# A two-stage macaron block with routed experts: results scattered to token rows, low halves formed on VectorE

## The reference

```
x = x + 0.5 * ffn0(norm(x))         # gate, up 256 -> 1024, silu(gate)*up, down
x = x + attn0(norm(x))              # 16 heads of 128, 4 key heads, window mask, rotary
x = x + 0.5 * ffn0(norm(x))
x = x + 0.5 * moe(norm(x))          # the same weights both times
x = x + attn1(norm(x))              # 16 heads of 16, causal, rotary
x = x + 0.5 * moe(norm(x))
```

## Time and profile before

| | us |
|---|---|
| median of 3 runs (890.39 to 892.46) | 890.73 |
| the profiled execution | 887.51 |
| its span, first to last instruction | 885.7 |
| PE busy (share of span) | 722.8 (82%) |
| DVE busy | 621.2 (70%) |
| ACT busy | 454.4 (51%) |
| POOL busy | 397.9 (45%) |

### The profile page before, as it was taken

How to read it: one execution, slowest core, us unless ns; L and a number is a source line. 1 busy time by engine, 2 the same in 40 slices (tenths; PEclk the granted TensorE clock), 3 DMA queues, 4 the chain that set the end, 5 groups by cost and what they waited for, 6 DMA issues and landing times. The chain is left out here.

```text
span 885.7 us, 17508 instructions
## 1 busy us (share of the span) xinstructions
PE 722.8 (82%) x5515; PEld 487.4 (55%) x5515; DVE 621.2 (70%) x1376; ACT 454.4 (51%) x1033; POOL 397.9 (45%) x401
## 2 busy tenths in 40 slices
PE   6889789999889999698976887664896798758883
PEld 3555357777456777354543555333785685436642
DVE  5989868777867787699756554534888695835535
ACT  3435667787667786364322454224666473314531
POOL 4644856766756665385444420743007301230025
PEclk8999989999999999999988899876898698979986
DMA  9999000000000000300001332200000100023313
GB/s 374 316 418 411 23 0 1 0 0 1 1 1 0 0 0 1 113 1 1 24 25 47 95 99 78 83 19 1 1 2 1 48 2 1 1 84 102 103 58 121
DMA packets 36432, 58.83 MB, mean 66 GB/s; under 512 B 11026, under 2 KB 28562, under 8 KB 35858
## 3 DMA queue, kind: packets, MB, share of 16 engines
q1 hardware_dynamic: 32866, 49.49, 15.5%
q0 software_dynamic: 3072, 8.39, 3.0%
q10 hardware_dynamic: 432, 0.15, 0.1%
HBM read 27.87 MB, written 30.15 MB: 66 GB/s over the span
## 5 line engine op out<-in xcount | busy, mean ns | idle before, releaser
L1458 PE MATMUL PS<-XT,WA 128*128 128x512 f16 x432 | 101.1, 382 | 0.0
L603 POOL TENSOR_TENSOR ARENA<-ARENA,ST 128x512 f32<-128x512 f32 x64 | 66.6, 1041 | 67.8 <-DVE ST L1248 67.8
L714 ACT ACTIVATE ARENA<-T 128x512 f16<-128x512 f32 (+1 forms) x56 | 35.2, 629 | 105.1 <-DVE T L1142 90.8
L1458 PE MATMUL PS<-WA,ARENA 128*128 128x256 f16 (+2 forms) x960 | 70.3, 215 | 15.2 <-DVE ARENA L1151 14.2
L1458 PEld LDWEIGHTS PS<-WA,ARENA 128*128 128x128 f16 x960 | 57.6, 98 | 31.4 <-DVE ARENA L1151 18.8
L1458 PE MATMUL PS<-XT,WC 128*128 128x512 f16 x264 | 67.7, 411 | 6.5 <-DVE T L1135 5.2
L561 POOL DMA_INDIRECT WA<-ys_rows,IDX x16 | 17.3, 1081 | 114.4 <-DMA ys_rows<-WA 110.1
L1458 PEld LDWEIGHTS PS<-XT,WA 128*128 128x128 f16 (+1 forms) x432 | 42.7, 99 | 45.0 <-issue 1.9
L1458 PE MATMUL PS<-KVR,ARENA 128*128 (+1 forms) x384 | 59.3, 283 | 6.4 <-DVE ARENA L1220 4.1
L1228 DVE TENSOR_REDUCE ST<-PS 128x2 f32<-128x512 f32 x64 | 44.0, 687 | 28.8 <-PE PS L1458 28.0
L747 ACT ACTIVATE ARENA<-PS,ST 128x256 f32<-128x256 f32 x128 | 59.4, 471 | 8.6 <-DVE ST L1231 8.4
(11 more groups left out here) (179 smaller groups left out, 1839.2 us busy)
## 6 DMA issues: line engine op xcount, KB each, us to landing
xs_rows<-ROUT SPq DMA_DIRECT2D x1, 9216.0 KB, 26.6
ys_rows<-ROUT SPq DMA_DIRECT2D x1, 9216.0 KB, 48.9
WA<-xs_rows SPq DMA_DIRECT2D x46, 128.0 KB, 2.0
ys_rows<-WA SPq DMA_DIRECT2D x46, 128.0 KB, 1.7
WB<-wb_dram SPq DMA_DIRECT2D x1, 4096.0 KB, 21.8
WC<-wc_dram SPq DMA_DIRECT2D x1, 2304.0 KB, 26.9
WA<-wa_dram SPq DMA_DIRECT2D x4, 512.0 KB, 7.6
WA<-wa_dram SPq DMA_DIRECT2D x1, 2048.0 KB, 13.1
```

The costliest lines, as they stand in the source:

```text
L603: pl.tensor_tensor(pr, pr, rs.broadcast_to([P, 2, S]), ALU.mult).then_inc(norm_done, 1)
L714: sc.activation(HH[r, a, 0, :], T3[r, :], ACT.Copy).then_inc(hid_hi, 1)
L1458: ins = te.matmul(dst, left(a), right(b), start=first and n == 0, stop=last and n == 2, skip_group_check=True)
```

## The change

1. Results go straight to rows by token. Each row of the table now carries two more numbers (ROW = D + 2): the token's first expert and twice its number. POOL scatters a block's results (`results(m, b)`) with one indirect DMA to yt_rows, row 2*token + (0 or 1), the target being made by one VectorE instruction per block (`target`). SP's stores and POOL's 16 gathers go; SP loads YG in four plain DMAs. The tables xs_rows are now two, one per moe, filled before with zeros and free row numbers (FREE); ys_rows and its fill go.
2. VectorE forms all low halves of the shared expert; POOL's share (L535) goes. POOL's scatter of the first half moves to step 1 of glu(2, 0), that of the second half behind glu(2, 0) or glu(3, 0).
3. Routing: slots move to step 5, the block table (`routing_table`) to step 0 of glu(f, 1) and the second half's weights to its step 1; PE's prefix goes behind that step's down.
4. The order within an expert iteration changes on PE, ACT and VectorE.
5. PRE is 3 for the second moe. n splits start at step 4 (N_AT) of glu(1, 0), those left over share glu(1, 1)'s first steps. The d splits stand in every second iteration, i = 2 to 16.

```diff
-PRE = 2
+PRE = {2: 2, 3: 3}
+ROW = D + 2
...
+        DIX = sb("DIX", [P, 24], I32)
+        IDP = sb("IDP", [P, ROWS // P + TT], I32)
+        FREE = sb("FREE", [P, ROWS // P], F32)
...
-        SIXTH = [("g", j) for j in range(JF - JS, E)] + [("n", j) for j in range(JF - 2, E)]
+        SIXTH = [("g", j) for j in range(JF - JS, E)]
+        N_AT = 4
...
-            ORDER += [FIFTH[step]] + ([("n", step - 2)] if step >= 2 else [])
-        ORDER += SIXTH + [("d", j) for j in range(8)]
+            ORDER += [FIFTH[step]] + ([("n", step - N_AT)] if step >= N_AT else [])
+        for step in range(JF):
+            ORDER += SIXTH[step:step + 1] + ([("n", step + JF - N_AT)] if step + JF - N_AT < E else [])
+        ORDER += [("d", j) for j in range(8)]
...
@@ SP @@
-            for table in (XS, YS):
-                sp.dma_start(table.rearrange("(p a r) d -> p a (r d)", p=P, r=4),
-                             ROUT[:, 0:4 * D].rearrange("p (o n) -> p o n", o=1)
-                             .broadcast_to([P, ROWS // P // 4, 4 * D])).then_inc(dma_z, 16)
+            sp.wait_ge(base_set, 5)
+            for table in XS:
+                t3 = table.rearrange("(a p) d -> p a d", p=P)
+                sp.dma_start(t3[:, :, 0:D + 1], ROUT[:, 0:D + 1].rearrange("p (o n) -> p o n", o=1)
+                             .broadcast_to([P, ROWS // P, D + 1])).then_inc(dma_z, 16)
+                sp.dma_start(t3[:, :, D + 1:ROW], FREE[:, :].rearrange("p (a o) -> p a o", o=1),
+                             allow_slow_non_contiguous=True).then_inc(dma_z, 16)
...
+                for b in range(NBK):
                     g = NBK * m + b
-                    at[b] = sp.value_load(TBL[0:1, 1, b:b + 1], min_val=0, max_val=ROWS // P - 1)
+                    row = sp.value_load(TBL[0:1, 1, b:b + 1], min_val=0, max_val=ROWS // P - 1)
                     after(sp, xb_turned, g - 2)
-                    sp.dma_start(XB[:, g % 3, :], XS[ds(at[b] * P, P), :]).then_inc(xb_in[g % 3], 16)
-
-                def store(b):
-                    g = NBK * m + b
-                    sp.wait_ge(ye_copied, g + 1)
-                    sp.dma_start(YS[ds(at[b] * P, P), :], YB[:, g % 3, :]).then_inc(yb_out[g % 3], 16)
-
-                for b in range(NBK + 6):
-                    if b < NBK:
-                        load(b)
-                    if b >= 6:
-                        store(b - 6)
+                    after(sp, dix_done, g - 2)
+                    sp.dma_start(XB[:, g % 3, :], XS[m][ds(row * P, P), :]).then_inc(xb_in[g % 3], 16)
+                for i in range(3):
+                    sp.wait_ge(yb_out[i], 16 * slot_total(i, m))
+                for u in range(NB):
+                    sp.dma_start(YG[u // UPH][:, u % UPH], YT[2 * ROWS + 4 * P * u:2 * ROWS + 4 * P * (u + 1), :]
+                                 .rearrange("(t p k) d -> p t k d", t=2, k=2)).then_inc(gathered[u], 16)
...
@@ POOL @@
-            def gather(m):
...
+            def results(m, b):
+                g = NBK * m + b
+                pool.wait_ge(ye_copied, g + 1)
+                pool.wait_ge(dix_done, g + 1)
+                pl.indirect_dma_start(YT, bass.IndirectOffsetOnAxis(ap=DIX[:, b:b + 1], axis=0), YB[:, g % 3, :], None,
+                                      bounds_check=2 * ROWS + 2 * TOK - 1).then_inc(yb_out[g % 3], 16)
...
             run_glu(pool, 2, 0, glu_step, glu_side)
-            for b in range(8):
-                if b < 4:
-                    prepare1(b)
-                split(*split_d(b))
-            gather(0)
+            scatter(3, 1)
+            for i in range(4):
+                prepare1(i)
+            for b in range(NBK):
+                results(0, b)
+                if 2 <= b < 18 and b % 2 == 0:
+                    split(*split_d(b // 2 - 1))
...
@@ ACT @@
-                if (f, hf) == (1, 0) and j == 2:
+                if (f, hf) == (1, 0) and j == N_AT:
                     act.wait_ge(dma_n, 16 * len(pieces(KH)))
...
                         gate_tanh(i)
+                    if 1 <= i <= NBK:
+                        hidden_high(i - 1)
                     if i >= 2:
                         result(i - 2)
                     if i + 2 < NBK:
                         tokens_high(i + 2)
-                    if 1 <= i <= NBK:
-                        hidden_high(i - 1)
-                    if m == 0 and 2 <= i < 10:
-                        split(*split_d(i - 2))
+                    if m == 0 and 2 <= i < 18 and i % 2 == 0:
+                        split(*split_d(i // 2 - 1))
...
@@ DVE @@
+                link(v.tensor_tensor(SLB, EQ[:, 0], KB[:, 0:E].rearrange("p (o e) -> p o e", o=1)
+                                     .broadcast_to([P, TPH, E]), ALU.mult))
+                first = XN[:, UPH * hf:UPH * hf + UPH, :, D:D + 1].rearrange("p u t n -> p (u t) n")
+                link(v.tensor_reduce(first, SLB, AX.X, ALU.add))
                 v.tensor_copy(IDX[:, :, TPH * hf:TPH * hf + TPH], SF).then_inc(idx_done, 1)
...
-                if not low_on_pool(f, hf):
-                    dve.wait_ge(hid_hi, st + 1)
-                    v.tensor_tensor(HH[r, a, 1, :], T3[r, :], HH[r, a, 0, :], ALU.subtract).then_inc(hid_lo, 1)
+                dve.wait_ge(hid_hi, st + 1)
+                v.tensor_tensor(HH[r, a, 1, :], T3[r, :], HH[r, a, 0, :], ALU.subtract).then_inc(hid_lo, 1)
...
+                def target(b):
+                    g = NBK * m + b
+                    dve.wait_ge(xb_in[g % 3], 16 * (slot_uses(g) + 1))
+                    v.scalar_tensor_tensor(DIX[:, b:b + 1], XB[:, g % 3, D:D + 1], BLK[:, 0, b:b + 1],
+                                           XB[:, g % 3, D + 1:D + 2], ALU.not_equal, ALU.add).then_inc(dix_done, 1)
...
                         hidden(i)
-                    if i + 2 < NBK:
-                        tokens_low(i + 2)
                     if 1 <= i <= NBK:
                         hidden_low(i - 1)
-                    if m == 0 and 2 <= i < 10:
-                        split(*split_d(i - 2))
+                    if i + 2 < NBK:
+                        target(i + 2)
+                        tokens_low(i + 2)
+                    if m == 0 and 2 <= i < 18 and i % 2 == 0:
+                        split(*split_d(i // 2 - 1))
...
@@ PE @@
                         gate_up(i)
+                    if 1 <= i <= NBK:
+                        turn_hidden(i - 1)
                     if i >= 2:
                         project(i - 2)
                     if i + 2 < NBK:
                         turn_tokens(i + 2)
-                    if 1 <= i <= NBK:
-                        turn_hidden(i - 1)
```

More of the change, by code:

```diff
@@ L531, in glu_step @@
                     split(*x)
-                if low_on_pool(f, hf):
-                    pool.wait_ge(hid_hi, st + 1)
-                    r = rows(f, j)
-                    pl.tensor_tensor(HH[r, a, 1, :], T3[r, :], HH[r, a, 0, :], ALU.subtract).then_inc(hid_lo, 1)
             def glu_side(f, hf, j):
@@ L665, in _ @@
             run_glu(pool, 3, 0, glu_step, glu_side)
-            gather(1)
+            scatter(6, 1)
+            for b in range(NBK):
+                results(1, b)
         @block.scalar
@@ L702, in glu_step @@
                 after(act, gated, st)
-                if f >= 2 and hf == 1 and j == PRE:
+                if f >= 2 and hf == 1 and j == PRE[f]:
                     act.wait_ge(gu_gated, NBK * (f - 1))
@@ L1197, in hidden_low @@
                                     HTB[:, g % 2, 0], ALU.subtract).then_inc(htb_lo, 1)
-                tokens_low(0)
-                tokens_low(1)
+                def target(b):
[3 more added lines that the diff above has]
+                                           XB[:, g % 3, D + 1:D + 2], ALU.not_equal, ALU.add).then_inc(dix_done, 1)
+                for b in range(2):
+                    target(b)
+                    tokens_low(b)
                 for i in range(NBK + 2):
@@ L1436, in _ @@
             glu(2, 0)
-            glu(2, 1, (0, PRE))
+            glu(2, 1, (0, PRE[2]))
             expert_blocks(0)
-            glu(2, 1, (PRE, JS))
+            glu(2, 1, (PRE[2], JS))
             turn_norm(4, 0)
@@ L1443, in _ @@
             glu(3, 0)
-            glu(3, 1, (0, PRE))
+            glu(3, 1, (0, PRE[3]))
             expert_blocks(1)
-            glu(3, 1, (PRE, JS))
+            glu(3, 1, (PRE[3], JS))
             for u in range(UPH, NB):
@@ L1552, in step @@
                         ins.then_inc(up_done, 1)
-                    if HOSTED[f, hf] in ROUTED and j == 4:
-                        prefix(*HOSTED[f, hf])
                     if start:
@@ L1557, in step @@
                         clear(hf)
-                    elif not (f >= 2 and hf == 1 and j == PRE):
+                    elif not (f >= 2 and hf == 1 and j == PRE[f]):
                         down(f, hf, j - 1, 1 - a, st - 1)
+                    if HOSTED[f, hf] in ROUTED and j == 4:
+                        prefix(*HOSTED[f, hf])
```

(13 more changed lines are left out.)

92 lines of the change are left out of this document (47 added, 45 removed).

## The result

The changed kernel takes 861.33 us (median of 4 runs, 858.86 to 866.04), the kernel before 890.56: the ratio is 0.9679, 95% interval 0.9632 to 0.9727. The forecast was 859.9, between 851 and 874.

What follows compares the result with a forecast made beforehand. It took PE to be near its bound in the first stage but held by waits, the blocks by a ring between engines. Gains summed to 30.8 us, off the 890.7 median: 859.9, own range 853 to 867, other cases 851 to 874.

Steps and rivals of the forecast that it cites:

- a: glu(1, 0): n splits moved from step 2 to step 4, so the wait for the down weights goes; 5.7 us gained.
- b: glu(1, 1): down product ahead of prefix fills PE's wait for the mask, and the clock falls less; 2.2 us gained.
- c: glu(2, 0) to the blocks: low halves on VectorE, no stall behind POOL's scatters, blocks start earlier; 7.0 us gained.
- d: Expert blocks: new order cuts the ring project, turn_tokens, tokens_high, tokens_low, hidden_low; period 2.475 to 2.05; second stage gains 9.8 us.
- Rival 1: The ring stays, or moved waits close another through target or PE's register loads; period 2.48, total 873.6 us; chance 0.16.
- e: First expert stage: ScalarE's d splits wait for POOL's behind scatters, block pairs take 6.2 us; 4.9 us lost altogether.
- f: After the first stage: plain loads replace POOL's gathers, so roots and both norms come earlier; 3.7 us gained.
- g: glu(3, 0) and second stage's start: later indices, earlier scatter, one more covered GLU step; first gate_up within 1 us, 0 gained.
- Attention 1: Attention 1: two links added on its path; 0.4 us lost.
- h: The end, behind the last block: one GLU step fewer and no waiting for gathers, 25.1 against 32.8 us; 7.7 gained.
- Rival 5: The fill's 4-byte elements hold up routing from 0.27 us each, all gain gone from 0.30; chance 0.04.
- The rule weighed: VectorE in a two-port mode locks out GpSimd's descriptor writes, making POOL's scatter per block wrong; 4.5 us, chance 0.10.

Runs made afterwards that it cites:

- variant 3: The changed kernel with N_AT = 2, the n splits and the wait for the down weights back at step 2 of glu(1, 0): ratio 0.9769.
- variant 2: The changed kernel with POOL making d split j right behind the scatter of result 2j, not 2j + 2: 852.23 us, ratio 0.9592.
- variant 7: The changed kernel with the low halves of glu(2, 0) alone back on POOL: ratio 0.9776.
- variant 1: The changed kernel with the old order of PE, ScalarE and VectorE in the expert blocks: ratio 0.984.
- variant 5: The changed kernel with PE loading all 23 expert numbers by 23 loads ahead of the first block, not one per block: ratio 0.9863.
- variant 10: The changed kernel with one load instruction for the 23 expert numbers ahead of the blocks, range checks kept: ratio 0.9749.
- variant 12: The changed kernel with the edits of variant 2, variant 10 and variant 6 together, without the range checks: 829.99 us, ratio 0.9384.
- variant 6: The changed kernel with the low halves of glu(3, 0) alone back on POOL: ratio 0.9675.
- variant 4: The changed kernel with PRE = 2 for the second stage, one GLU step back from the scatters' cover to the end: ratio 0.9729.
- variant 8: The changed kernel with the second routing's first-half scatters moved from attention 1 to step 1 of glu(3, 0): ratio 0.9709.

## Why the prediction was right, and where it was not

- **a, right.** 5.7 forecast with the splits' cost in it, 4.94 measured: 5.64 in glu(1, 0), less 0.70 (not 1.8) for the four splits (variant 3).
- **b, wrong: 2.2 forecast, 0.1 measured.** The step that failed: "The down product (1.3 us until PE takes the next) goes into the 2.17 us wait". It does, but I didn't ask who is late next: PE waits for the low half instead (2.3 us). That VectorE sets the steps there fits its 31.2 busy us of the 34.4 of glu(1, 1) in variant 3, but PE is busy as long, so it is inferred from the waits. The 0.9 for the clock isn't borne out either: in glu(2, 0) it stayed at 1.00 behind a wait of 2.14 us in variant 2, and fell behind one of 2.14 in variant 3.
- **c, right in size** (7.0; 6.8 and 0.5), with the mechanism as forecast: no stall behind scatters, the scatter 0.86 us behind its index cast (457.86 to 458.72), the blocks 15.35 behind the scatter's start. Variant 7 shows that it is the stall, not the order of the table, and rival 4 falls with the 7.33 gained.
- **d, right mechanism, wrong size: 9.8 forecast, 5.65 measured.** The ring was cut (variant 1). "PE's 2.0 becomes the bound; I take 2.05" failed: 2.0 is what PE's products need (variants 5, 10, 12), but PE's queue also holds a register load and two checks between gate_up and turn_hidden, which stood ahead of a wait before and so seemed free there. Load and checks together cost 0.28 us a block (6.4 / 23). Rival 1 named PE's register loads; of the 9.8 us that it would have taken from the second stage they took 4.15.
- **e, right.** Pairs of 6.2 forecast, 6.21 measured; -4.9 and -4.11. Variant 2 shows the cause. Rivals 2 and 3 fall: the scatters took 0.97 to 1.02 us, and POOL started them 0.77 to 0.84 behind the result.
- **f, right**: 3.7 and 4.52. PE's gap ahead of the norms' turn fell from 10.93 to 7.02. The stretch took 23.3 to 23.5 us in the profiles beside 890 us and 21.78 in the others; the difference is that of the first 24 products again (6.89 to 7.04 us against 5.35).
- **g, right in sum** (0 and 0.72), by two terms that cancel: low halves on VectorE cost 3 us (variant 6), and more of the scatters is covered by a step.
- **Attention 1, wrong**: -0.4 and -6.35. The step that failed is the term itself: it counted two links and nothing else. 4.44 lie in the open question above; in the eight other profiles the whole loss was 0.6 to 2.5 us.
- **h, undersized: 7.7 and 10.44.** From the last product's end to the program's end I had 7.7 us; it is 7.48 (852.12 to 859.6). What failed is "it ends near 17.4": it ended 14.9 behind the last result. (20.8 less the step's 3.9 is 16.9, not 17.4, so half a microsecond is a slip in the sum.) What makes the difference is the clock behind the stage, which I had left as it was: 24 products in 5.35 us instead of 7.92 (shown with variant 4), a term put at nothing without a reason, and one that not all variants gain. Variant 4 gives 2.5 to 3.8 us for the step (I took 3.9).
- **Rival 5, the fill, falls.** Each column of 9,216 elements landed 48 us after its issue, beside the wide part, the last near 136 us, where the routing's ranks come behind 400. That is 576 elements for each of 16 engines, at most 0.08 us each, where it decides from 0.27:

```profile
L466 SPq DMA_DIRECT2D xs_rows<-ROUT x2: 767/9178/17590, 41.6 to 69.9; - x2
L468 SPq DMA_DIRECT2D xs_rows<-FREE x2: 27392/28198/29005, 42.4 to 87.5; - x2
```

- **The rule weighed**: a scatter per block beside a busy VectorE was not the wrong engine's work. One argument there was empty: no scatter ran beside the block rows, so that none of them is longer says nothing. The group of the results' scatters (count, busy us, mean ns):

```profile
L558 POOL DMA_INDIRECT yt_rows<-WA,DIX x46 | 45.3, 984 | 79.4 <-ACT WA L846 47.9
```

They took 984 ns in the mean, while VectorE was busy 64% of the second stage. The lock that the Trainium skill describes (SBUF — State Buffer, Who interferes with whom) doesn't show in these rows. Of the 32 scatters to xs_rows some still took up to 1.29 us (1.755 before), and no run tells what stretches those.

## What to carry to other kernels

When a ring between engines is cut, price what the next bound holds in its own queue, register loads and their range checks included: they are not in the busy time, and they are free only ahead of a wait. Work of an engine that only helps (a split of weights) belongs ahead of whatever waits in its queue for the pipeline, never behind it, if an engine of the pipeline waits for that work. And where PE's wait is filled by moving its own work into it, ask first which wait comes next: another engine, here busy 90% of the stretch, may set the step anyway.

And before a gain is booked to an edit, look at the same stretch in every kernel that leaves it alone. Here the start, attention 1 and the end each moved by 3 to 7 us with nothing edited in them.

## What the runs showed of the hardware

- A register load with its two range checks on PE's queue: up to 0.85 us each in a row of 23, and 0.28 us a block in a loop, behind a matmul group of 1.06 us. A single load of 23 numbers without checks delays PE by nothing that shows.
- The same stretch of glu(2, 0) kept a granted clock of 1.00 through PE's waits of 2.14, 1.72 and 2.70 us in variant 2, and fell to 0.66 over 10 us behind one of 2.14 in variant 3; the stretch took 48.3 and 51.9 us.
- The same 24 products behind the second stage took 7.92 us at a granted clock of 0.67 before the change, 5.35 at 1.00 in the changed kernel and 6.99 in variant 8, which edits nothing there.
- The kernel before took 890.1 us in one set of runs, 880.8 in the next and 882.7 in a third, about 1%. The ratios compare over sets (0.9679 and 0.9696 for the changed kernel); single stretches need care, for attention 1 took 170.1 us in one profile of the changed kernel and 165.95 in another.
